# Second attention of a four-layer kernel: late row maxima, the doubts' branch, and a larger VectorE share of the first batch's counts

## The chip, the cores and the metric

The kernel runs on one core of a Trainium2 chip. The metric is the device time of one execution in microseconds (us), as the median of a few runs. TensorE is called PE here, VectorE DVE, ScalarE ACT, GpSimd POOL, SyncE SP.

## What is computed

Four layers, each attention then feed-forward, each with adaptive layer norm and a gated residual. The change lies in the attention of the second layer. It keeps, in every row of probabilities, the `k_keep` largest of 256, where `k_keep` is a number per head:

```python
q, k, v = (proj(Wq, bq), proj(Wk, bk), proj(Wv, bv))
scores = jnp.einsum('bhqd,bhkd->bhqk', q, k) / jnp.float32(np.sqrt(dh))
attn = jax.nn.softmax(scores, axis=-1)
k_keep = jnp.maximum(1, (L * (1.0 - sr)).astype(jnp.int32))
order = jnp.argsort(-attn, axis=-1)
rank = jnp.argsort(order, axis=-1)
keep = rank < k_keep[None, :, None, None]
w = jnp.where(keep, attn, jnp.float32(0.0))
w = w / (jnp.sum(w, axis=-1, keepdims=True) + 1e-10)
out = jnp.einsum('bhqk,bhkd->bhqd', w, v)
```

The batch is 8, there are 16 heads of 8 values, and 256 tokens; x is 8 x 256 x 128 in float32.

## The kernel before

The second attention, `l1_attn`, treats one batch entry after the other. Tokens lie on the 128 partitions, two tiles of them, so a batch has ROWS1 = 32 "rows", one for each head and token tile, each 128 x 256 probabilities. Instead of a sort it searches a threshold for each row and token. For batch b:

- PE computes the scores of head h (`l1_scores`, L1734) into one of three PSUM banks; DVE takes the negative row maximum (`l1_max`, L3092, tile `nmax`); ACT writes the exponentials and their sums (`l1_exps`, L4213). Scores of head h wait for the exponentials of head h - 3.
- After head 15's maximum, POOL makes the argument of a guessed threshold (`ask_start`, L1116), and ACT takes its exponential (`l1_start`, L4247).
- Three passes count in each row how many probabilities lie below the threshold (`QUICK_STEPS` = 3). DVE counts the first ROWS_DVE = 6 rows (`count_below`, L3105), ACT the other 26 with a Sign activation (`l1_count`, L4263). ACT's count of signs is in other units, so aim, window and the like (`keep_below`, `aim_below`, `per_count`, ...) are kept per row, with a factor 1 for DVE's rows and 2 for ACT's (`by_engine`). After each pass DVE moves the thresholds: `first_move` (L3113), `second_move` (`narrow`, L3125, and `between`), `settle_on` (`narrow`, `between` and some more). Each waits for ACT's counts, `counts_act`.
- DVE marks and counts what lies below the settled threshold in all 32 rows (`count_kept`, L3176), and works out how many of at most 8 are left over in each row. If a row has more, it is in doubt: `doubt` sums this, PE adds it over the partitions (`l1_doubt`), `ask_doubt` reads it (L3197), and `settle_doubt` branches on it (register load L3204, branch L3206, code after it from L3212). The branch skips a slow bisection, which these inputs do not need.
- POOL multiplies out candidates of a group of 4 rows (`candidates`), DVE takes the 8 largest of each (`largest_of`, L3220), and removes those that are too many (`all_but_past`, `mark`, L3232). PE turns kept probabilities to keys-first (`l1_turn_probs`, L1749 and L1750), ACT copies them (`l1_take_probs`, L4274), PE weighs the values (`l1_weigh`, L1762), ACT copies each four heads (`l1_take_quad`, L4278), and the batch is projected out.

Nothing is scheduled by a program: each engine has its own `l1_attn` with a loop `for n in range(-1, B)`, whose body interleaves by hand the batches n (marking and weighing), n + 1 (counting), n + 2 (scores and maxima) and n + 3 (norm and projection: `l1_norm`, L4222, `l1_turn`, L1676). `now(i)` says that batch i exists. Each engine works strictly in the order written, and waits on semaphores. In iteration -1 there is nothing to mark yet. `l1_gates` (L3041 to L3046) turns the modulation of all batches to gates, once. `l1_keep_counts` makes the limits per row, once, before the attention; its five instructions per engine share are L2954 to L2958.

DVE's loop, where row maxima and counts alternate:

```python
if now(n + 1):
    count_kept(n + 1, 8, 16)
if now(n + 2):
    l1_max(n + 2, 13)
    l1_max(n + 2, 14)
    l1_max(n + 2, 15)
if now(n + 1):
    count_kept(n + 1, 16, 24)
    count_kept(n + 1, 24, 32)
```

## Time and profile before

| | us |
|---|---|
| median of 3 runs | 2033.48 (2032.08 to 2033.51) |
| the profiled execution, its own time | 2029.82 |
| its span in the trace | 2028.1 |
| PE busy | 1561.3 (77%) |
| DVE busy | 1480.3 (73%) |
| ACT busy | 1123.5 (55%) |
| POOL busy | 877.5 (43%) |

Busy times are over the whole span, in which the second attention takes roughly from 489 to 1070 us. Rows give the start and the duration of an instruction in us from the span's start; in square brackets stands how long the engine was idle before it, and whose work ended that. "DVEq" and "ACTq" are the engines' sequencers, which handle branches, register loads and plain semaphore increments. Tile names are those of buffers that the program uses again: ACT's signs go to `rope_c` and `rope_s`, the counts of DVE to `scale_b`, `gate_b` and two more, and `weights`, `big`, `O` and `kT` hold probabilities.

### The profile page before, as it was taken

What the parts mean: (1) busy time and instruction counts of PE and PEld (TensorE: products, weight loads), DVE (VectorE), ACT (ScalarE), POOL (GpSimd) and SP (SyncE); (2) the same over time, 40 slices, a digit from 0 to 9 for tenths busy, and PEclk for the clock granted to TensorE, in tenths of its full rate; (3) what the DMA queues carried; (4) which work ended last, traced back from release to release, by engine and by line L of the source; (5) the groups of instructions that cost most, each with busy time, mean ns of one, the idle gap of its engine ahead of it and who ended that gap; (6) DMA issues with size and microseconds to landing.
All of it is one profiled execution on the core that took longest, in us unless ns stands there. A gap on an engine that the chain in (4) does not pass through costs nothing.

```text
span 2028.1 us, 38143 instructions
## 1 busy us (share of the span) xinstructions
PE 1561.3 (77%) x12256; PEld 997.2 (49%) x12256; DVE 1480.3 (73%) x4763; ACT 1123.5 (55%) x3354; POOL 877.5 (43%) x1162
## 2 busy tenths in 40 slices
PE   3878989987347777776669788527777799999978
PEld 3445667675223343343336556313443477777763
DVE  6678766555589999999998742458876778887657
ACT  2444444445988998999853333114452377666620
POOL 3333221124244554455333677666200377767610
PEclk8889999997567877878778989758896899999969
DMA  4111101003000000000001033222120000000000
GB/s 139 47 47 43 41 19 43 19 2 123 15 9 17 13 10 12 17 9 9 1 1 59 31 89 106 90 70 69 47 89 1 15 1 1 2 1 2 1 1 21
DMA packets 67303, 67.53 MB, mean 33 GB/s; under 512 B 9956, under 2 KB 58967, under 8 KB 66567
## 3 DMA queue, kind: packets, MB, share of 16 engines
q1 hardware_dynamic: 58930, 53.09, 8.0%
q0 software_dynamic: 5120, 10.50, 2.0%
q8 instruction: 101, 1.65, 0.3%
q10 hardware_dynamic: 3040, 1.38, 0.2%
q14 instruction: 112, 0.91, 0.1%
HBM read 30.41 MB, written 8.39 MB: 19 GB/s over the span
## 4 chain that ended last, share of the span: by engine, by line
PE 35%; ACT 22%; DVE 20%; issue 9%; POOL 6%; SPq 4%; ACTq 2%; DMA 1%; DVEq 0%; POOLq 0%; another core or an unknown queue 0%
ACT rope_s L4263 5%; ACT rope_c L4263 5%; POOL weights L1170 4%; SPq L694 4%; DVE weights L3176 3%; PE bank L2163 3%; PE bank L1556 3%; PE bank L2123 3%; ACT big L4485 3%; PE bank L1572 3%; DVE nmax L2731 2%; PE bank L2150 2%; PE bank L2111 2%; ACTq L4096 2%; DVE nmax L3092 2%
## 5 line engine op out<-in xcount | busy, mean ns | idle before, releaser
L2731 DVE TENSOR_REDUCE nmax<-bank 128x4 f32<-128x1024 f32 x144 | 175.9, 1222 | 51.5 <-PE bank L1336 48.4
L1762 PE MATMUL bank<-probsT,V 128*9 128x256 f32 x512 | 156.3, 450 | 28.4 <-ACT probsT L4274 28.3
L896 POOL TENSOR_TENSOR big<-big,rinv 128x512 f32<-128x512 f32 x128 | 131.6, 1048 | 45.7 <-DVE rinv L3795 45.7
L4078 ACT ACTIVATE feat_o<-bank 128x1024 f32<-128x1024 f32 x72 | 73.7, 1023 | 103.4 <-PE bank L1336 75.4
L4078 ACT ACTIVATE O<-bank 128x1024 f32<-128x1024 f32 x72 | 73.7, 1024 | 98.5 <-PE bank L1336 71.8
L3789 DVE TENSOR_REDUCE nmax<-bank 128x2 f32<-128x512 f32 x128 | 82.0, 683 | 58.1 <-PE bank L2123 58.1
L4485 ACT ACTIVATE big<-bank,nmax 128x256 f32<-128x256 f32 x256 | 117.6, 477 | 11.1 <-DVE nmax L3789 11.1
L4493 ACT ACTIVATE big<-bank 128x512 f32<-128x512 f32 x128 | 73.8, 614 | 68.8 <-PE bank L2150 68.8
L1750 PE MATMUL bank<-silu_b,weights 128*128 128x128 bf16 x464 | 108.6, 256 | 0.0
L1170 POOL DMA_INDIRECT weights<-h_rows,V x96 | 91.7, 955 | 32.2 <-issue 28.9
L1734 PE MATMUL bank<-qT 48*128 48x256 bf16 x256 | 53.9, 346 | 62.0 <-ACT weights L4213 42.5
L4274 ACT ACTIVATE probsT<-bank 128x512 f32<-128x512 f32 x128 | 76.1, 601 | 39.4 <-PE bank L1750 21.3
L3092 DVE TENSOR_REDUCE nmax<-bank 128x2 f32<-128x512 f32 x128 | 84.1, 681 | 9.8 <-PE bank L1734 9.8
L1762 PEld LDWEIGHTS bank<-probsT,V 128*9 128x9 f32 x512 | 39.0, 98 | 98.8 <-ACT probsT L4274 40.1
L2163 PE MATMUL bank<-big,V 128*64 128x256 f32 x512 | 69.4, 390 | 16.8 <-ACT V L4500 15.7
L3565 DVE TENSOR_TENSOR O<-O,bank 128x512 f32<-128x512 f32 x24 | 16.5, 688 | 90.0 <-ACT O L4409 88.4
L1749 PE MATMUL bank<-const,big 128*128 128x128 f32 x256 | 68.1, 347 | 17.4 <-ACT probsT L4274 11.4
L4137 ACT ACTIVATE hid<-bank,weights 128x256 f32<-128x256 f32 x128 | 52.5, 470 | 48.6 <-PE bank L1556 48.5
L2150 PE MATMUL bank<-const,big 128*128 128x128 f32 x512 | 75.0, 279 | 2.5 <-POOL big L896 1.7
L1178 POOL DMA_INDIRECT weights<-y_rows,V x64 | 62.0, 968 | 29.7 <-issue 16.9
L1360 PE MATMUL bank<-big 57*128 57x128 bf16 (+1 forms) x512 | 41.7, 266 | 39.6 <-DVE nmax L2731 22.6
L2150 PEld LDWEIGHTS bank<-const,big 128*128 128x128 f32 x512 | 56.6, 141 | 28.9 <-issue 16.5
(821 smaller groups left out, 5094.5 us busy)
## 6 DMA issues: line engine op xcount, KB each, us to landing
qT<-parts SPq DMA_DIRECT2D x276, 32.0 KB
big<-V SPq DMA_DIRECT2D x192, 32.0 KB
y_rows<-weights SPq DMA_DIRECT2D x24, 256.0 KB, 2.2
big<-parts SPq DMA_DIRECT2D x180, 32.0 KB
weights<-in_weights_l_ffn SPq DMA_DIRECT2D x1, 4832.0 KB, 14.4
weights<-in_weights_l_attn SPq DMA_DIRECT2D x1, 3904.0 KB, 13.2
qT<-V SPq DMA_DIRECT2D x96, 32.0 KB
weights<-in_weights_l_ffn SPq DMA_DIRECT2D x1, 2860.0 KB, 11.4
```

Of the source, the lines that this page charges most:

```text
L896: nc.gpsimd.tensor_tensor(row, row, rinv[:, h % H, :].unsqueeze(2).to_broadcast([P, T, S]), ALU.mult).then_inc(scaled.sem, 1)
L1170: nc.gpsimd.indirect_dma_start(gathered[i % RING1][:, t, :], None, h_rows, bass.IndirectOffsetOnAxis(ap=token_of[:, at:at + 1], axis=0)).t ...
L1750: last = mm(pb[6 + h % 2][:, at], unkept(b, g)[:, 2 * (h % 2) + t, keys], minus_two, start=False, stop=True)
L1762: last = mm(pb[1][part, 0:S].rearrange("p (t n) -> p t n", t=T), values_of(b, k)[:, h * wide:(h + 1) * wide], by_keys[:, k], start=k == 0, ...
L2150: last = nc.tensor.transpose(pb[TURN_BANKS3[h % 2]][:, k * S + t * P:k * S + (t + 1) * P], probs3[h % PROBS3][:, t * S + k * P:t * S + (k ...
L2163: last = mm(pb[7][HD3 * i:HD3 * (i + 1), w * S:(w + 1) * S], values3(q, k, 2 * w + i), probsT3[(4 * q + 2 * w + i) % TURNED3][:, k * S:(k ...
L2731: V_.tensor_reduce(to, scored.rearrange("p (i a n) -> p i a n", i=HPG, n=n), AX.X, ALU.max, negate=True).then_inc(score_max.sem, 1)
L3092: V_.tensor_reduce(nmax[:, h, :], tiles(pb[2 + n % 3]), AX.X, ALU.max, negate=True).then_inc(max_ready.sem, 1)
L3789: V_.tensor_reduce(nmax[:, h % H, :], tiles(pb[h % 4][:]), AX.X, ALU.max, negate=True).then_inc(max_ready.sem, 1)
L4078: nc.scalar.activation(turned_probs[n % TURNS], turned_scores, ACT.Exp).then_inc(turned_exp.sem, 1)
L4263: nc.scalar.activation(signs[signed[0] % len(signs)], row_of(b, j), ACT.Sign, bias=at[:, 0, j:j + 1], scale=-1.0, accum_out=at[:, 1, j:j + ...
L4485: last = nc.scalar.activation(probs3[h % PROBS3][:, t * S:(t + 1) * S], pb[h % 4][:, t * S:(t + 1) * S], ACT.Exp, bias=nmax[:, h % H, t:t ...
```

## The change

- DVE counts 14 rows for batch 0 (`ROWS_FIRST`) and 6 for the others; ACT counts the rest, 18 and 26. The limits per row are first made for 14 and 18, and once batch 0 has settled, `resplit_rows` makes them again for 6 and 26: ten instructions, each waiting for the one before. POOL makes `per_count` again in `start_ends` of batch 1.
- `l1_gates` moves from before the loop to between the second count of batch 0 and its `second_move`.
- The maximum of head 0 of batch n + 2 moves from behind the first `mark` to between the two `largest_of` that precede the branch of the doubts; PE computes these scores right after `l1_doubt`.
- The maxima of heads 13, 14 and 15 are spread over `count_kept`, four rows of it before each.
- PE's `l1_turn` of batch n + 3 follows the first `l1_turn_probs`.
- ACT's first count from row 20 on is in one piece, and `l1_norm` follows it.

```diff
@@ -52,7 +52,7 @@
 ROWS1 = H * T
-ROWS_DVE = 6
+ROWS_DVE, ROWS_FIRST = 6, 14
 GROUPS = ROWS1 // 4
@@ -65,7 +65,7 @@
 BISECT_RAISES = 5
-KEEP_STEPS = 32
+KEEP_STEPS, RESPLIT_STEPS = 32, 10
@@ -484,7 +484,8 @@
         window_below, per_count = (masks_flat[:, ROWS1 * i:ROWS1 * (i + 1)] for i in range(2))
-        by_engine = ((slice(0, ROWS_DVE), 1.0), (slice(ROWS_DVE, ROWS1), 2.0))
+        rows_dve = lambda b: ROWS_DVE if b else ROWS_FIRST
+        by_engine = lambda b: ((slice(0, rows_dve(b)), 1.0), (slice(rows_dve(b), ROWS1), 2.0))
         silu1 = tail1[:, 0:B * P].rearrange("p (b n) -> p b n", b=B)
@@ -1086,7 +1087,7 @@
                 link(nc.gpsimd.memset(start_half[:], 0.5))
-                for of, each in by_engine:
+                for of, each in by_engine(0):
                     link(nc.gpsimd.memset(per_count[:, of], DAMPED / (PSEUDO * each)))
@@ -1119,6 +1120,10 @@
                 step = guesses[b % 3][:, 1, :]
+                if b == 1:
+                    for of, each in by_engine(b):
+                        link(nc.gpsimd.memset(per_count[:, of], DAMPED / (PSEUDO * each)))
+                    pool.wait_ge(keep_count, KEEP_STEPS + RESPLIT_STEPS)
                 pool.wait_ge(start_ready.sem, start_ready(ph, b, 1))
@@ -1806,18 +1811,19 @@
                         l1_doubt(n)
+                    if now(n + 2):
+                        l1_scores(n + 2, 0)
                     if now(n - 1):
                         l1_turn_quad(n - 1, QUADS - 1)
                     if now(n + 2):
                         l1_values(n + 2)
-                    if now(n + 3):
-                        l1_turn(n + 3)
-                    if now(n + 2):
-                        l1_scores(n + 2, 0)
                         l1_scores(n + 2, 1)
                         l1_scores(n + 2, 2)
                     if now(n):
                         l1_turn_probs(n, 0)
+                    if now(n + 3):
+                        l1_turn(n + 3)
+                    if now(n):
                         l1_turn_probs(n, 1)
@@ -2914,6 +2920,28 @@
+            def split_rows(b, then):
+
+                for of, each in by_engine(b):
+                    then(V_.tensor_scalar(keep_below[:, of], keep[:, of], -each, float(S), ALU.mult, ALU.add))
+                    then(V_.tensor_scalar(aim_below[:, of], aim[:, of], -each, float(S), ALU.mult, ALU.add))
+                    then(V_.tensor_scalar(under_below[:, of], aim_below[:, of], -each * PSEUDO, None, ALU.add))
+                    then(V_.tensor_scalar(over_below[:, of], aim_below[:, of], each * PSEUDO, None, ALU.add))
+                    then(V_.memset(window_below[:, of], each * each * ((LEFT / 2) ** 2 + 0.3)))
+
+            def resplit_rows():
+
+                dve.wait_ge(mid_ready.sem, mid_ready("l1_attn", 0, QUICK_STEPS))
+                n = [KEEP_STEPS]
+
+                def then(ins):
+                    n[0] += 1
+                    ins.then_inc(keep_count, 1)
+                    dve.wait_ge(keep_count, n[0])
+
+                split_rows(1, then)
+                assert n[0] == KEEP_STEPS + RESPLIT_STEPS, f"RESPLIT {n[0]}"
+
             def l1_keep_counts(ph="l1_attn"):
@@ -2950,12 +2978,7 @@
                 then(V_.tensor_scalar(aim[:], keep[:], -LEFT / 2, None, ALU.add))
-                for of, each in by_engine:
-                    then(V_.tensor_scalar(keep_below[:, of], keep[:, of], -each, float(S), ALU.mult, ALU.add))
-                    then(V_.tensor_scalar(aim_below[:, of], aim[:, of], -each, float(S), ALU.mult, ALU.add))
-                    then(V_.tensor_scalar(under_below[:, of], aim_below[:, of], -each * PSEUDO, None, ALU.add))
-                    then(V_.tensor_scalar(over_below[:, of], aim_below[:, of], each * PSEUDO, None, ALU.add))
-                    then(V_.memset(window_below[:, of], each * each * ((LEFT / 2) ** 2 + 0.3)))
+                split_rows(0, then)
                 aim_of = aim[:].rearrange("p (h t) -> p h t", t=T)[:, :, 0]
@@ -3096,10 +3119,10 @@
                     dve.wait_ge(start_ready.sem, start_ready(ph, b, 1))
-                    dve.wait_ge(probs_ready.sem, probs_ready(ph, b, (ROWS_DVE + 1) // 2))
+                    dve.wait_ge(probs_ready.sem, probs_ready(ph, b, (rows_dve(b) + 1) // 2))
                 else:
                     dve.wait_ge(mid_ready.sem, mid_ready(ph, b, it))
-                for j in range(ROWS_DVE):
+                for j in range(rows_dve(b)):
                     if j >= len(flags):
@@ -3290,19 +3313,19 @@
                 l1_spread(1)
                 l1_guess(1)
-                l1_gates()
                 for n in range(-1, B):
                     if now(n + 1):
                         count_below(n + 1, 0)
                     if now(n):
                         ask_doubt(n)
                         largest_of(n, 0)
+                    if now(n + 2):
+                        l1_max(n + 2, 0)
+                    if now(n):
                         largest_of(n, 1)
                         settle_doubt(n)
                         all_but_past(n, 0)
                         mark(n, 0)
-                    if now(n + 2):
-                        l1_max(n + 2, 0)
                     if now(n + 1):
                         first_move(n + 1)
@@ -3332,6 +3355,8 @@
                         count_below(n + 1, 1)
+                        if n < 0:
+                            l1_gates()
                         second_move(n + 1)
@@ -3365,6 +3390,8 @@
                     if now(n + 1):
                         settle_on(n + 1)
+                    if n + 1 == 0:
+                        resplit_rows()
                     if now(n + 2):
                         l1_max(n + 2, 9)
@@ -3374,14 +3401,19 @@
                         l1_max(n + 2, 12)
                     if now(n + 1):
-                        count_kept(n + 1, 8, 16)
+                        count_kept(n + 1, 8, 12)
                     if now(n + 2):
                         l1_max(n + 2, 13)
+                    if now(n + 1):
+                        count_kept(n + 1, 12, 16)
+                    if now(n + 2):
                         l1_max(n + 2, 14)
+                    if now(n + 1):
+                        count_kept(n + 1, 16, 20)
+                    if now(n + 2):
                         l1_max(n + 2, 15)
                     if now(n + 1):
-                        count_kept(n + 1, 16, 24)
-                        count_kept(n + 1, 24, 32)
+                        count_kept(n + 1, 20, 32)
                     if now(n + 3):
                         l1_guess(n + 3)
@@ -4256,7 +4288,7 @@
                     act.wait_ge(probs_ready.sem, probs_ready(ph, b, (end - 1) // T + 1))
-                for j in range(first, end):
+                for j in range(max(first, rows_dve(b)), end):
                     signed[0] += 1
@@ -4286,11 +4318,9 @@
                     if now(n + 1):
-                        l1_count(n + 1, 0, 20, 21)
+                        l1_count(n + 1, 0, 20, ROWS1)
                     if now(n + 3):
                         l1_norm(n + 3)
-                    if now(n + 1):
-                        l1_count(n + 1, 0, 21, ROWS1)
                     if now(n):
```

(Left out: the start number of steps in `l3_route`, which follows the ten new ones.) Three places in the order of DVE's instructions, before and after. First iteration -1, from the guess of batch 1 on: L3078 is its last instruction, L3041 to L3046 (now L3064 to L3069) are the gates, L3105 (now L3128) is one counted row, and `nmax` a maximum. Before:

```order
L3078 TENSOR_SCALAR hb<-hb 128x32
L3041 TENSOR_SCALAR hid<-bank 128x1024
L3042 TENSOR_SCALAR hid<-bank 128x1024
L3044 TENSOR_TENSOR hid<-bank,hid 128x1024
L3046 SCALAR_TENSOR_TENSOR probs<-hid 128x1024
L3105 TENSOR_SCALAR scale_b,front_n<-big,front_n 128x256
L3105 TENSOR_SCALAR gate_b,front_n<-big,front_n 128x256
```

And now, the end of the second count, the gates, and the second `narrow`:

```order
L3128 TENSOR_SCALAR gate_sign,small<-big,small 128x256
L3128 TENSOR_SCALAR scale_b,small<-big,small 128x256
L3128 TENSOR_SCALAR gate_b,small<-big,small 128x256
L3064 TENSOR_SCALAR hid<-bank 128x1024
L3065 TENSOR_SCALAR hid<-bank 128x1024
L3067 TENSOR_TENSOR hid<-bank,hid 128x1024
L3069 SCALAR_TENSOR_TENSOR probs<-hid 128x1024
L3148 TENSOR_TENSOR small<-small,routes 128x32
L3149 TENSOR_TENSOR small<-small,routes 128x32
```

The gates have left the place ahead of the first count and stand ahead of the second `narrow`; each count has 14 such rows instead of 6. Next the last maxima in iteration 3; L3164 (now L3187) ends `settle_on`, L3176 (now L3199) is `count_kept`. Before:

```order
L3164 COPY_PREDICATED small<-small 128x32
L3092 TENSOR_REDUCE nmax<-bank 128x2 x2
L3176 TENSOR_SCALAR weights,small<-big,small 128x256 x8
L3092 TENSOR_REDUCE nmax<-bank 128x2 x2
L3176 TENSOR_SCALAR weights,small<-big,small 128x256 x8
L3092 TENSOR_REDUCE nmax<-bank 128x2 x3
L3176 TENSOR_SCALAR weights,small<-big,small 128x256 x12
L3176 TENSOR_SCALAR O,small<-big,small 128x256 x4
```

And now:

```order
L3187 COPY_PREDICATED small<-small 128x32
L3115 TENSOR_REDUCE nmax<-bank 128x2 x2
L3199 TENSOR_SCALAR weights,small<-big,small 128x256 x8
L3115 TENSOR_REDUCE nmax<-bank 128x2 x2
L3199 TENSOR_SCALAR weights,small<-big,small 128x256 x4
L3115 TENSOR_REDUCE nmax<-bank 128x2
L3199 TENSOR_SCALAR weights,small<-big,small 128x256 x4
L3115 TENSOR_REDUCE nmax<-bank 128x2
L3199 TENSOR_SCALAR weights,small<-big,small 128x256 x4
L3115 TENSOR_REDUCE nmax<-bank 128x2
```

Of the last three maxima, each now stands behind four more counted rows than the one before it, and head 15's behind row 19. Last, the branch of the doubts in iteration 3; MAX is `largest_of`, L3204 (now L3227) the register load. Before:

```order
L3197 CAST doubts_i<-bank 1x1
L3199 MEMSET gap 128x1
L3220 MAX small<-hid 128x8 x8
L3204 TENSOR_LOAD doubts_i
L3204 ISA x2
L3206 COMPARE_AND_BRANCH
```

And now:

```order
L3220 CAST doubts_i<-bank 1x1
L3222 MEMSET gap 128x1
L3243 MAX small<-hid 128x8 x4
L3115 TENSOR_REDUCE nmax<-bank 128x2
L3243 MAX small<-hid 128x8 x4
L3227 TENSOR_LOAD doubts_i
L3227 ISA x2
L3229 COMPARE_AND_BRANCH
```

A maximum has come between the two groups of four MAX.

## Rows read from the trace of the kernel before

**Rows 1.** The page: busy us, share of the span, instructions, of two engines.
```profile
PE 1561.3 (77%) x12256; PEld 997.2 (49%) x12256; DVE 1480.3 (73%) x4763; ACT 1123.5 (55%) x3354; POOL 877.5 (43%) x1162
```
**Rows 2.** Timeline of ACT: `l1_start` and first signs (start, us, what, idle before).
```profile
637.16 0.23 ACT L4247 ACTIVATE front_n<-neg_mid 128x32 f32<-128x32 f32 x1 [0.62 <-POOL neg_mid L1117]
...
776.95 0.51 ACT L4263 ACTIVATE rope_c<-big,front_n 128x256 bf16<-128x256 f32 x1
...
777.46 0.49 ACT L4263 ACTIVATE rope_s<-big,front_n 128x256 bf16<-128x256 f32 x1
...
984.24 0.23 ACT L4247 ACTIVATE front_n<-neg_mid 128x32 f32<-128x32 f32 x1 [0.61 <-POOL neg_mid L1117]
```
**Rows 3.** Busy time by engine in two windows of one period.
```profile
776.69:832.29 55.60, 42.44 (x209) 22.25 (x208) 50.80 (x218) 54.56 (x209) 28.88 (x38) 0.72 0.04 12
832.29:845.78 13.49, 10.52 (x62) 4.99 (x62) 13.16 (x57) 9.71 (x37) 4.50 (x4) 0.87 0.05 13
```
Columns: stretch, its length, busy time (instructions) of PE, PE's weight loads, DVE, ACT and POOL, granted clock, DMA share, GB/s.

**Rows 4.** Timeline of ACT in the same period: its waits.
```profile
786.28 0.38 ACT L4278 ACTIVATE V<-bank 128x256 f32<-128x256 f32 x1 [0.57 <-PE bank L1762]
...
794.98 0.60 ACT L4274 ACTIVATE probsT<-bank 128x512 f32<-128x512 f32 x1 [0.17 <-ACT rope_s L4263]
...
840.22 0.47 ACT L4213 ACTIVATE weights<-bank,nmax 128x256 f32<-128x256 f32 x1 [2.22 <-DVE nmax L3092]
...
844.62 0.47 ACT L4213 ACTIVATE O<-bank,nmax 128x256 f32<-128x256 f32 x1 [1.49 <-DVE nmax L3092]
...
846.53 0.23 ACT L4247 ACTIVATE front_n<-neg_mid 128x32 f32<-128x32 f32 x1 [0.62 <-POOL neg_mid L1117]
```
**Rows 5.** Timeline of DVE and POOL around the last maxima of that period.
```profile
843.90 1.88 DVE L3092 TENSOR_REDUCE nmax<-bank 128x2 f32<-128x512 f32 x3
845.69 0.47 DVE L3176 TENSOR_SCALAR_CACHE_REDUCE weights<-big,small 128x256 bf16<-128x256 f32 x1
...
845.86 0.25 POOL L1116 TENSOR_TENSOR neg_mid<-hb,nmax 128x32 f32<-128x32 f32 x1 [1.64 <-DVE nmax L3092]
...
846.09 0.47 DVE L3176 TENSOR_SCALAR_CACHE_REDUCE weights<-big,small 128x256 bf16<-128x256 f32 x1
```
**Rows 6.** Timeline of DVE: `first_move`, second and third `narrow` of that period.
```profile
794.88 0.19 DVE L3113 TENSOR_TENSOR front_n<-front_n,routes 128x32 f32<-128x32 f32 x1 [1.38 <-ACTq L4267]
...
812.40 0.19 DVE L3125 TENSOR_TENSOR small<-small,routes 128x32 f32<-128x32 f32 x1 [0.56 <-ACTq L4267]
...
832.29 0.18 DVE L3125 TENSOR_TENSOR small<-small,routes 128x32 f32<-128x32 f32 x1
```
**Rows 7.** Timeline of DVE: behind the branch, iterations 1 and 3, and head 0.
```profile
651.84 0.43 DVE L3212 TENSOR_TENSOR weights<-const,small 128x256 f32<-128x256 f32 x1 [2.02 <-DVEq L3209]
...
790.51 0.43 DVE L3212 TENSOR_TENSOR weights<-const,small 128x256 f32<-128x256 f32 x1 [1.16 <-DVEq L3209]
...
792.82 0.68 DVE L3092 TENSOR_REDUCE nmax<-bank 128x2 f32<-128x512 f32 x1
```
**Rows 8.** Timeline of DVE and ACT in iterations -1 and 0.
```profile
514.05 1.22 DVE L3041 TENSOR_SCALAR hid<-bank 128x1024 f32<-128x1024 f32 x1 [2.96 <-PE bank L1664]
...
536.85 0.19 DVE L3125 TENSOR_TENSOR small<-small,routes 128x32 f32<-128x32 f32 x1 [4.65 <-ACTq L4267]
...
553.73 0.19 DVE L3125 TENSOR_TENSOR small<-small,routes 128x32 f32<-128x32 f32 x1 [3.78 <-ACTq L4267]
...
581.82 0.42 DVE L3212 TENSOR_TENSOR weights<-const,small 128x256 f32<-128x256 f32 x1 [1.65 <-DVEq L3209]
...
585.84 0.60 ACT L4274 ACTIVATE probsT<-bank 128x512 f32<-128x512 f32 x1 [2.13 <-PE bank L1750]
```
**Rows 9.** Timeline of DVE: ten limits per row in `l1_keep_counts`, and the next.
```profile
444.47 0.17 DVE L2954 TENSOR_SCALAR routes<-keep 128x6 f32<-128x6 f32 x1
...
446.43 0.17 DVE L2960 TENSOR_SCALAR gate_b<-aim 128x16 f32<-128x16 f32 x1
```

2 lines of the change are left out of this document (1 added, 1 removed).

## Prediction

> **What bounds the kernel now.** I began with the page [rows 1]: VectorE is busy 73% of the span and ScalarE 55%, which says nothing about the second attention, since both figures are means over nine stages. So I went to the instructions in order of time. `l1_start` (line 4247) runs once per batch, and its rows give the period: from 637.16 us (batch 2) to 984.24 us (batch 7) there are five batches, (984.24 - 637.16) / 5 = 69.4 us each [rows 2]. Next I cut one period into three windows [rows 3]. From `l1_start` of one batch (776.69) to VectorE's third `narrow` (832.29), ScalarE is busy 54.56 of 55.60 us. Its only long wait there is 0.57 us for PE's last weighing [rows 4]; the rest are the 0.17 us pauses at the end of its counts. From 832.29 to 845.78 VectorE is busy 13.16 of 13.49 us, while ScalarE waits 2.22 and 1.49 us for row maxima. Then GpSimd's `ask_start` waits for the last maximum, takes 0.6 us, and `l1_start` follows at 846.53 [rows 4, 5].
>
> So the loop that sets the period is: last row maximum (VectorE), `ask_start` (GpSimd), `l1_start` and all three passes of counting (ScalarE), third `narrow` and everything up to the last row maximum (VectorE). Its parts are 55.6 + 13.5 + 0.75 (845.78 to 846.53) = 69.8 us for this batch. VectorE has slack outside its part of the loop: 1.38 us before `first_move`, 0.56 us before the second `narrow`. Only at the third `narrow`, 832.29, do both arrive together; no wait stands in its row [rows 6].
>
> **The change, part by part.** The sum is against the profiled execution, 2029.82 us (span 2028.1); the runs' median, 2033.48, lies 3.7 us above, and I add that at the end.
>
> 1. *Late maxima.* Before, the maxima of heads 13, 14 and 15 ran together at 843.90 to 845.78, before row 16 of `count_kept` [rows 5]. Now maximum 15 stands behind rows 16 to 19 as well. The rows of that count start 0.40 us apart (845.69, 846.09 [rows 5]), so four make 1.61 us. Everything that hangs on maximum 15 comes 1.61 us later: `ask_start`, `l1_start`, and with them ScalarE's 55 us. The head 13 maximum comes earlier by 1.6 us, so ScalarE's wait before `l1_exps` of head 13 (1.49 us) goes; but behind it stands only `l1_take_quad`, and then `l1_start`, so that time reappears as a wait for `l1_start`: 0.62 before, about 3.7 us now. VectorE loses nothing at first, it does the same work in another order, but its slack behind it fills with waiting for ScalarE. The late starts are those of batches 2 to 7, six of them (iterations 0 to 5): 6 x 1.61 = **+9.7 us**. That of batch 1 is also late, by 1.61 less what part 2 gains, but there ScalarE has 2.13 us to spare at 585.84 [rows 8], which covers it.
>
> 2. *First batch.* VectorE counts 14 rows instead of 6, ScalarE 18 instead of 26. ScalarE's rows start 0.50 us apart (776.95, 777.46 [rows 2]), so a pass costs it 4.0 us less; VectorE's 8 more rows cost 3.2 us where it waited 4.65 and 3.78 us [rows 8]. I followed it through. Pass one: VectorE needs no longer wait for `l1_gates` (514.05 after 2.96 us of waiting, then four instructions of 1.22 us, 4.9 us in all [rows 8]); it counts at once from 511.1, where that wait began, so `first_move` falls at about 517.4, after 14 rows and a maximum, where before the gates alone lasted until 518.9. Pass two: ScalarE counts until about 528.4, but VectorE counts until 527.9 and then does the 4.9 us of `l1_gates`, so the second `narrow` starts at 532.8 instead of 536.85. Pass three: with 2.1 us for `narrow` and `between` and 5.7 for 14 rows VectorE is done at 540.7, and only then come the statistics and maximum 5, out at 542.3, for which ScalarE now waits some 5 us in the middle of its count; its last 14 rows then take it to about 550.5. The third `narrow` starts there instead of at 553.73: 3.2 us are left. Then come the ten new instructions of `resplit_rows`, each behind the last; the same ten took 1.96 us (444.47 to 446.43 [rows 9]), 2.05 with the first wait. What is left is **-1.15 us**. It passes through VectorE to the first `mark`, and from there to ScalarE, which waits for it [rows 8]. The two memsets and the wait added to GpSimd's `start_ends` of batch 1 are free: the next to need it is `first_move`, 10 us on.
>
> 3. *Branch of the doubts.* The maximum of head 0 moves from behind the first `mark` to between the two `largest_of` (0.6 us, 792.82 [rows 7]). The first `mark`, for which PE's `l1_turn_probs` and then ScalarE wait, comes 0.6 us later, unless the branch hides it. Branch and register load cost VectorE 1.16 us here after the eighth MAX8, and 2.02 us in batch 1 [rows 7]. No row tells whether the load starts while MAX8 still runs. Bounds: if it does, the extra maximum lies in its shadow and the cost is 0. If not, 0.6 us in iterations 0, 1 and 5, where ScalarE waits for PE at this point, and the 0.6 less some 0.3 of slack in 2 to 4 (from the first instruction behind the branch to ScalarE took 585.84 - 581.82 = 4.02 us where it waited [rows 8]; 790.51 + 4.02 = 794.53, against 794.98 found [rows 4, 7]): 2.7 us. The rows favour neither, I take half: **+1.4 us**.
> The Trainium skill (TensorE: Matmul & The Clock Gate, on engine queue depths) gives VectorE a strictly ordered queue of 8, so that the sequencer can be ahead of the engine by about those MAX8. By that rule the load is under way early, and this term would be 0 and the sum 1.4 us lower; no row here shows it.
>
> 4. *ScalarE's count in one piece.* `l1_norm` moves behind the first pass. The counts are out 0.87 us earlier, `first_move` waits less, but ScalarE's work up to the second `narrow` is the same, and VectorE waits there for the rest: 0. If VectorE were the bound, this would be a gain (below).
>
> 5. *PE.* Scores of batch n+2 no longer stand behind `l1_turn`, which waits for the branch; ScalarE's first exponentials never waited for them (the maximum is out at 793.5, and ScalarE is still at its count and then at `l1_take_probs` until 795.5 [rows 4, 7]), so 0. `l1_turn` now follows `l1_turn_probs` of head 0 and may hold `l1_take_normed` by 0 to 0.2 us a batch, 1 us in all; I take 0, as ScalarE's copy of the probabilities (0.60 us [rows 4]) covers the two transposes.
>
> Sum: +9.7 - 1.15 + 1.4 = +9.9 us, 2039.7 us for a profiled execution, **2043.4 us** for the median of the runs.
>
> **Rivals.**
> - *VectorE sets the period* (faster). Then the maxima's place is free, the count in one piece takes 0.87 us off the wait at `first_move` in each of six batches, and the branch hides 0.6 us in seven: 5.2 + 4.2 + 1.15 = 10.6 us less, 2022.9 for the median. It decides if ScalarE has room for 1.6 us between `l1_start` and the third `narrow`. For it: VectorE arrives there without waiting in one batch. Against it: ScalarE is busy 98% of that window, and VectorE waits for it twice a batch. Chance 0.08.
> - *The lateness is absorbed* (no change). VectorE's waits, 1.38 + 0.56 us, are more than 1.61, and if ScalarE could catch up inside a period, only the first batch's -1.15 would show: 2032.3. Against it: an engine that works in order and is 98% busy catches up only by its 1.0 us of waits, most of which move with it. Chance 0.10.
> - *The branch gets dearer* (slower still). The gap after MAX8 was 1.65 and 2.02 us in the first two batches and 1.16 in the fourth, with the same instructions each time [rows 7, 8]. If the shifted code makes it 2.02 everywhere, that is 0.86 us more in six batches, less 0.3 of slack in half of them: +4.3 us, 2047.7. Chance 0.12. The Trainium skill (Runtime: NRT & Kernel Launch, on instruction fetch) says that a taken branch to a target outside the fetched pages stalls for a fetch, which would make such a gap hang on where code lies; the scatter here agrees with it but does not prove it.
> - *The first batch does not gain at all*: its part is 1.15 us, and the forecast's range holds it.
>
> **How the numbers follow.** A measurement of this kernel can tell 0.2%, about 4 us, from no change. My forecast has 0.70, and the dearer branch 0.12: 0.82 for slower. The absorbed case gives 0.10 for within 0.2%, the VectorE case 0.08 for faster. The forecast's own bounds: down 1.4 (hidden branch) and one late start absorbed, 1.6, so 2040.4; up 1.3 + 1.0 and 0.6, so 2046.3. The base adds uncertainty: the profiled time lay 3.7 us below the median, so an offset may be as small as 0 and the low end 2036.7. With the dearer branch above, the range is 2036.5 to 2048; it leaves out the faster and the absorbed case, 0.18.
>
> **What would show it.** In the changed profile: rows of `l1_start` about 71.0 to 71.5 us apart instead of 69.4, with some 3.7 us of ScalarE waiting for GpSimd before each; VectorE waiting over 1.5 us more per batch in sum before `first_move`, `narrow` and the reading of the doubts; third `narrow` of batch 0 near 550.5, and the maximum after it near 555.4; the gap behind the last MAX8 of batch 1 on at 1.2 us (not hidden) or 0.6 us (hidden). I am wrong if the starts stay 69.4 us apart, or if ScalarE, started later, still finishes its third pass in time.

## The result, and the profile after

| | before | after |
|---|---|---|
| median of the runs, same chip | 2034.49 (2032.08 to 2037.95, 6 runs) | 2042.45 (2038.67 to 2047.55, 6 runs) |
| span of the profiled execution | 2028.1 | 2039.9 |

The ratio after to before is 1.0044, with a 95% interval of 1.0033 to 1.0055. The kernel got slower by some 8 to 9 us. The forecast was 9.9 us above a profiled execution of before, which gave 2039.7 for a profiled execution (2041.67 came out) and 2043.4 for the median. The page of after answers to [rows 1]:

```profile
PE 1560.6 (77%) x12256; PEld 996.6 (49%) x12256; DVE 1497.8 (73%) x4821; ACT 1112.7 (55%) x3306; POOL 878.3 (43%) x1164
```

Busy shares have not moved, and ScalarE even does 11 us less (24 counts of two instructions each fewer, in the first batch). What moved is the wait ahead of `l1_start`. The timeline of ACT after, against [rows 2]:

```profile
639.55 0.23 ACT L4279 ACTIVATE front_n<-neg_mid 128x32 f32<-128x32 f32 x1 [3.01 <-POOL neg_mid L1118]
...
783.12 0.23 ACT L4279 ACTIVATE front_n<-neg_mid 128x32 f32<-128x32 f32 x1 [2.50 <-POOL neg_mid L1118]
...
995.87 0.23 ACT L4279 ACTIVATE front_n<-neg_mid 128x32 f32<-128x32 f32 x1 [3.08 <-POOL neg_mid L1118]
```

Five periods take 356.32 us, 71.26 each instead of 69.42, and the wait for GpSimd is 2.5 to 3.1 us instead of 0.62 (the forecast had 3.7). Both come out of one place, which the timelines of DVE and POOL show (compare [rows 5]):

```profile
850.64 0.68 DVE L3115 TENSOR_REDUCE nmax<-bank 128x2 f32<-128x512 f32 x1
851.25 0.47 DVE L3199 TENSOR_SCALAR_CACHE_REDUCE weights<-big,small 128x256 bf16<-128x256 f32 x1
...
852.84 0.68 DVE L3115 TENSOR_REDUCE nmax<-bank 128x2 f32<-128x512 f32 x1
```
```profile
853.60 0.25 POOL L1117 TENSOR_TENSOR neg_mid<-hb,nmax 128x32 f32<-128x32 f32 x1 [3.24 <-DVE nmax L3115]
```

From head 14's maximum to head 15's it is 2.20 us, one maximum and four counted rows, where there were 0.6 us before. The windows of after follow: five periods, then, as in [rows 3], `l1_start` to the third `narrow` and from there to the last maximum (that of after is taken at its end, 853.53). Behind them stands the same five-period window of before:

```profile
639.55:995.87 356.32, 255.60 (x1348) 130.33 (x1348) 327.46 (x1360) 320.67 (x1227) 165.43 (x214) 0.79 0.04 11
783.12:838.42 55.30, 38.98 (x206) 20.17 (x204) 50.40 (x210) 54.55 (x209) 28.95 (x38) 0.81 0.04 12
838.42:853.53 15.11, 12.63 (x70) 6.11 (x70) 14.78 (x64) 9.83 (x37) 4.50 (x4) 0.77 0.04 11
```
```profile
637.16:984.24 347.08, 255.13 (x1349) 129.86 (x1348) 322.05 (x1360) 320.25 (x1227) 165.22 (x214) 0.79 0.04 11
```

The stretch up to the third `narrow` is as long as before (55.30 and 55.60 us, ScalarE busy 54.55 and 54.56). The one behind it went from 13.49 to 15.11 us: 1.62 us, where the working had 1.61. ScalarE's busy time over five periods is the same, 320.67 and 320.25 us; VectorE's is 5.4 us more, which the forecast had not (see the last section). Last, whose waits ScalarE has in these five periods, of before and of after (us in total, times, longest):

```profile
ACT big L4213 <- DVE nmax L3092: 7.4, 4, 2.2
ACT weights L4213 <- DVE nmax L3092: 6.6, 3, 2.2
ACT O L4213 <- DVE nmax L3092: 4.5, 3, 1.5
ACT front_n L4247 <- POOL neg_mid L1117: 3.7, 6, 0.6
ACT probsT L4274 <- PE bank L1750: 1.7, 2, 1.1
```
```profile
ACT front_n L4279 <- POOL neg_mid L1118: 17.3, 6, 3.1
ACT weights L4245 <- DVE nmax L3115: 6.6, 3, 2.2
ACT big L4245 <- DVE nmax L3115: 4.4, 2, 2.2
ACT O L4245 <- PE bank L1755: 2.4, 3, 0.9
ACT probsT L4306 <- PE bank L1755: 1.7, 2, 1.2
...
ACT big L4245 <- PE bank L1755: 1.3, 2, 0.7
ACT next_feat L4267 <- PE bank L1681: 0.9, 3, 0.3
```

The wait of `l1_start` grew by 13.6 us over the six starts counted; ScalarE's waits for row maxima fell from 18.5 to 11.0 us at the same time, since head 13's maximum comes earlier. The waits of `O` and `big` for PE are new, 3.7 us together: where ScalarE waited 1.49 us for a maximum it now waits 0.6 to 0.95 us for PE, and so the wait of `l1_start` is less than the forecast's 3.7 us. The last line is new too: three waits of 0.3 us for `l1_turn`.

### The profile page after: what moved, and what is told of

It reads as the page before. It is cut to its first block, busy times and chain, and to the rows that moved or that the text cites. A ratio compares the mean times of both kernels' runs of the same rounds, so it can differ in the third digit from the quotient of the medians.

```text
span 2039.9 us, 38150 instructions
## 1 busy us (share of the span) xinstructions
PE 1560.6 (77%) x12256; PEld 996.6 (49%) x12256; DVE 1497.8 (73%) x4821; ACT 1112.7 (55%) x3306; POOL 878.3 (43%) x1164
## 4 chain that ended last, share of the span: by engine, by line
PE 35%; DVE 22%; ACT 22%; issue 10%; POOL 6%; ACTq 3%; SPq 2%; DMA 1%; DVEq 0%; POOLq 0%
ACT rope_s L4295 5%; ACT rope_c L4295 5%; POOL weights L1175 4%; DVE weights L3199 3%; PE bank L2169 3%; PE bank L1561 3%; PE bank L2129 3%; ACT big L4515 3%; PE bank L1577 3%; ACTq L4128 2%; SPq L695 2%; DVE nmax L3115 2%; PE bank L2156 2%; PE bank L1390 2%; PE bank L2117 2%
## 5 line engine op out<-in xcount | busy, mean ns | idle before, releaser
L1754 PEld LDWEIGHTS bank<-const,big 128*128 128x128 f32 x256 | 45.1, 176 | 72.7 <-issue 36.6
L2156 PEld LDWEIGHTS bank<-const,big 128*128 128x128 f32 x512 | 56.6, 141 | 28.9 <-issue 16.5
```

The source lines that it names most:

```text
L1754: mm(pb[6 + h % 2][:, at], row_of(b, 2 * h + t)[:, keys], C("ident"), start=True, stop=False, is_transpose=True)
L2156: last = nc.tensor.transpose(pb[TURN_BANKS3[h % 2]][:, k * S + t * P:k * S + (t + 1) * P], probs3[h % PROBS3][:, t * S + k * P:t * S + (k ...
```

## The experiments

All but e2 and e12 are edits of the changed kernel, those two are edits of the kernel before. The diffs below are shortened to the calls that move, without their `if now(...)`. A "start" is a start of `l1_start`, the first interval is the time from start 0 to start 1, and a period is the time from one start to the next. The table has, from one profile of each kernel, the distance from `l1_start` of batch 0 to that of batch 7, and the mean of the last five periods. These are free of what happens ahead of the attention: its first `l1_start` fell anywhere from 502.3 to 511.0 us in these kernels.

| run | ratio to before (95%) | median | start 0 to 7 | period |
|---|---|---|---|---|
| before | 1 | | 479.56 | 69.42 |
| after | 1.0044 (1.0033 to 1.0055) | 2042.45 | 489.35 | 71.26 |
| e1 | 1.0003 (0.9990 to 1.0016) | 2034.18 | 480.98 | 70.14 |
| e2 | 1.0045 (1.0028 to 1.0062) | 2042.62 | 489.81 | 70.91 |
| e3 | 0.9978 (0.9966 to 0.9990) | 2029.80 | 474.74 | 69.24 |
| e4 | 1.0095 (1.0068 to 1.0121) | 2051.95 | 500.62 | 72.70 |
| e5 | 1.0049 (1.0032 to 1.0067) | 2044.53 | 489.01 | 71.24 |
| e6 | 1.0045 (1.0027 to 1.0063) | 2042.82 | 491.75 | 71.64 |
| e7 | 1.0050 (1.0032 to 1.0068) | 2041.51 | 489.18 | 71.27 |
| e8 | 1.0021 (1.0005 to 1.0036) | 2036.24 | 477.34 | 69.12 |
| e9 | 0.9962 (0.9948 to 0.9977) | 2027.88 | 475.24 | 69.30 |
| e10 | 0.9944 (0.9927 to 0.9960) | 2023.94 | 471.54 | 68.76 |
| e11 | 1.0086 (1.0070 to 1.0103) | 2053.36 | 496.69 | 72.65 |
| e12 | 0.9974 (0.9962 to 0.9985) | 2029.82 | 475.63 | 69.00 |

The kernel before had a median of 2033.29 beside e1 to e4, 2032.85 beside e5 to e8, and 2035.79 beside e9 to e12.

**e1, the changed kernel with the maxima put back.**

```diff
-count_kept(n + 1, 8, 12);  l1_max(n + 2, 13)
-count_kept(n + 1, 12, 16); l1_max(n + 2, 14)
-count_kept(n + 1, 16, 20); l1_max(n + 2, 15)
-count_kept(n + 1, 20, 32)
+count_kept(n + 1, 8, 16)
+l1_max(n + 2, 13); l1_max(n + 2, 14); l1_max(n + 2, 15)
+count_kept(n + 1, 16, 24); count_kept(n + 1, 24, 32)
```

> The changed kernel with the maxima of heads 13 to 15 back in one piece before row 16 of count_kept, all else as changed. Theory (the last maximum starts ScalarE's 55 us, nothing absorbs it): starts of ScalarE's first count back to about 69.4 to 69.7 us apart instead of 71.3, time 9.7 us below the changed kernel, about 2033, a little under the kernel before. Rival (the loss is in the other edits: PE's order, the branch, the count in one piece): starts stay 71 us apart and the time stays above 2040.

Measured: 2034.18, no change against before; the wait ahead of `l1_start` is back at 0.62 us. So nearly the whole loss hangs on the place of the maxima. Between starts 0 and 7 the late maxima cost 8.37 us here, against 10.25 in e2. The first interval is 2.42 us shorter than before (60.89 against 63.31), and yet start 0 to 7 is 1.4 us longer: the first batch's gain is given back on the way. The largest part, 2.46 us, is lost in the period in which VectorE stalls for 2.00 us behind the branch (iteration 4, see e7). The rest goes with waits of 0.3 to 0.6 us of ScalarE for PE, some of them where before had none. The granted clock over the five periods was 0.75 here and 0.79 in before, which is a second candidate for these waits (see the last section).

**e2, the kernel before with the late maxima alone** (the reverse of the diff above).

> The kernel before with the late maxima alone. Theory: 6 x 1.61 = 9.7 us above the kernel before, about 2044, starts 71.0 us apart. Rival (late maxima are absorbed, or hurt only together with the other edits): within 2 us of the kernel before, starts 69.4 apart.

Measured: 2042.62, as slow as the changed kernel. The period is 70.91 us, 1.49 above before. The late start of batch 1 (1.61 us) was not covered by ScalarE's 2.13 us to spare, as the working had it: at start 2 the delay is 2.79 us. VectorE's own path had moved as well. Counted from start 0, the doubts of batch 0 are read at 73.75 us (before 72.48), and ScalarE still waits 1.73 us for PE. The reading in e2, and in before:

```profile
581.61 0.14 DVE L3197 CAST doubts_i<-bank 1x1 int32<-1x1 f32 x1
```
```profile
577.16 0.14 DVE L3197 CAST doubts_i<-bank 1x1 int32<-1x1 f32 x1
```

One start on ACT's timeline, and the window over the five periods:

```profile
643.13 0.23 ACT L4252 ACTIVATE front_n<-neg_mid 128x32 f32<-128x32 f32 x1 [3.10 <-POOL neg_mid L1117]
```
```profile
643.13:997.67 354.54, 260.35 (x1348) 132.70 (x1348) 327.48 (x1360) 320.31 (x1226) 165.43 (x214) 0.77 0.04 11
```

VectorE's extra 5.4 us of busy time are here too (327.48), so they too belong to the maxima.

**e3, the maxima earlier than ever.**

```diff
 count_kept(n + 1, 8, 12)
 l1_max(n + 2, 13); l1_max(n + 2, 14); l1_max(n + 2, 15)
 count_kept(n + 1, 12, 32)
```

> The changed kernel with maxima 13, 14 and 15 together behind row 11 of count_kept, four rows earlier than in the kernel before and eight earlier than now. Theory: each row moved is worth 0.40 us a batch in both directions, so 6 x 3.2 = 19 us below the changed kernel, about 2023, starts 67.8 us apart. Rival (VectorE becomes the bound as soon as ScalarE starts earlier than in the kernel before): no more than 2 us below the kernel before, starts 69 us or more apart, ScalarE waiting for VectorE's threshold moves instead.

Measured: 2029.80, ratio 0.9978: faster than before, but by much less than eight rows a batch would be. ScalarE no longer waits at `l1_start`; it waits for PE at its first copy of probabilities (the waits of ACT, 633.93 to 980.11, and one of them on its timeline):

```profile
ACT probsT L4300 <- PE bank L1755: 8.9, 5, 3.0
```
```profile
791.11 0.60 ACT L4300 ACTIVATE probsT<-bank 128x512 f32<-128x512 f32 x1 [1.28 <-PE bank L1755]
```

The loop has changed hands. It now runs from the last maximum through the rest of `count_kept`, the doubts, their branch and the first `mark` (VectorE) to PE and ScalarE. Against the changed kernel the early maxima are worth 14.6 us between starts 0 and 7, about 2 us a batch of the 3.2 that the eight rows weigh.

**e4, the maxima four rows later still** (`count_kept` 16 to 24 ahead of maximum 15 in place of 16 to 20).

> The changed kernel with the maximum of head 15 another four rows later (behind row 23). Theory: another 6 x 1.61 = 9.7 us, about 2052, starts 72.9 us apart. Rival (most of the loss is a fixed cost of splitting the maxima, or of something else): within 3 us of the changed kernel.

Measured: 2051.95, and a period of 72.70. From start 0 to 7 it takes 11.27 us more than the changed kernel, 1.61 for each of seven batches; e2 took 10.25 more than before, 1.46 for each. On this side the price is nearly linear. One start:

```profile
641.38 0.23 ACT L4279 ACTIVATE front_n<-neg_mid 128x32 f32<-128x32 f32 x1 [4.69 <-POOL neg_mid L1118]
```

**e5, head 0's maximum back behind the first `mark`.**

```diff
 largest_of(n, 0)
-l1_max(n + 2, 0)
 largest_of(n, 1); settle_doubt(n); all_but_past(n, 0); mark(n, 0)
+l1_max(n + 2, 0)
```

> The changed kernel with the maximum of head 0 back behind the first mark (PE's order stays). Theory (the branch's register load runs while the eight MAX8 do, so the extra maximum is hidden): gap behind MAX8 back from 0.7 to 1.2-1.3 us, time from the CAST of the doubts to the code behind the branch unchanged at 4.3 us, starts 71.2 us apart as now, time within 2 us of the changed kernel (2042). Rival (the maximum costs its 0.6 us before mark): mark 0.6 us earlier in each batch, up to 3 us less.

Measured: the periods are those of the changed kernel within 0.2 us each, start 0 to 7 is 489.01 against 489.35. In iterations 1 to 5 VectorE's gap behind the eighth MAX8 is 1.14 to 1.30 us in place of 0.70 to 0.79. Iteration 2 in e5, then iteration 3 in the changed kernel:

```profile
724.69 0.14 DVE L3220 CAST doubts_i<-bank 1x1 int32<-1x1 f32 x1 [0.81 <-remote]
...
728.85 0.42 DVE L3235 TENSOR_TENSOR weights<-const,small 128x256 f32<-128x256 f32 x1 [1.14 <-DVEq L3232]
```
```profile
791.92 0.15 DVE L3220 CAST doubts_i<-bank 1x1 int32<-1x1 f32 x1
...
793.55 0.67 DVE L3115 TENSOR_REDUCE nmax<-bank 128x2 f32<-128x512 f32 x1
...
796.28 0.43 DVE L3235 TENSOR_TENSOR weights<-const,small 128x256 f32<-128x256 f32 x1 [0.74 <-DVEq L3232]
```

From the reading of the doubts (`CAST`) to the first instruction behind the branch it is 4.16 us without the maximum and 4.36 with it. Of its 0.6 us, 0.4 are hidden. The remaining 0.2 hardly show, since ScalarE's path is the longer one in most periods; in the three in which ScalarE waits for PE at its first copy, e5 is 0.22, 0.09 and 0.11 us shorter.

**e6, no larger share for batch 0** (six rows for all batches, no `resplit_rows`; `l1_gates` stays where the change put it).

> The changed kernel with 6 rows for VectorE in the first batch too, and no second making of the limits; the gates stay where the change put them. Theory 1 (moving the gates gives the first batch's gain; the larger share and its ten instructions cancel out): third narrow of batch 0 about 46.5 us after the first start, first maximum behind it as early as now (49.4 us after the first start), time within 1 us of the changed kernel. Theory 2 (the larger share is what gains): that maximum 2 us later. A stall of 1.8 us that now stands behind the branch in iteration 4 (waiting for nothing the profile shows) should move or go if it hangs on where code lies, as VectorE's program is shorter by 34 instructions there.

Measured: 2042.82, like the changed kernel. The first interval is 63.15 us; e2, which has the late maxima and nothing else, has 64.92, the changed kernel 62.49. So moving the gates, together with the small edits of PE's and ScalarE's order, which e6 keeps, gives 1.77 us, and the larger share adds 0.66. The later periods are 71.64 us, 0.38 above the changed kernel's; the granted clock over them was 0.74, against 0.79 there (see the last section). VectorE's stall of the changed kernel (see e7) stands in iteration 5 here, with 0.75 us. The third `narrow` in e6, then in the changed kernel, where the wait before it is hardly shorter:

```profile
554.33 0.19 DVE L3144 TENSOR_TENSOR small<-small,routes 128x32 f32<-128x32 f32 x1 [3.78 <-ACTq L4293]
```
```profile
551.06 0.19 DVE L3148 TENSOR_TENSOR small<-small,routes 128x32 f32<-128x32 f32 x1 [3.43 <-ACTq L4299]
```

**e7, 24 tiny memsets ahead of the loop**, which move VectorE's code.

```diff
 for h in range(H):
     l1_max(0, h)
+for _ in range(24):
+    linkup()
+    link(V_.memset(gap[:], 0.0))
+linkup()
```

> The changed kernel with 24 tiny memsets more on VectorE, where it waits for PE before the first batch's guess (2.9 us idle, so they cost under 0.5 us). Theory (the stall of 1.8 us in iteration 4 is the loading of code after the taken branch, and hangs on the program's position): it moves to another place or goes, and with it up to 1.3 us of the time. Rival (it belongs to what the instruction waits for): it stays at the same instruction with 1.8 us.

It tests a stall that the changed kernel shows in iteration 4 and the kernel before nowhere in this stretch. First the changed kernel, then e7:

```profile
867.39 0.42 DVE L3235 TENSOR_TENSOR weights<-const,small 128x256 f32<-128x256 f32 x1 [0.70 <-DVEq L3232]
869.61 0.23 DVE L3249 SCALAR_TENSOR_TENSOR small<-weights,small 128x64 f32<-128x64 f32 x1 [1.79 <-issue]
```
```profile
1065.27 0.23 DVE L3249 SCALAR_TENSOR_TENSOR small<-weights,small 128x64 f32<-128x64 f32 x1 [1.72 <-issue]
```

With the code shifted, the stall leaves iteration 4 and stands in iteration 7. In e1, e3 and e4, which have as many VectorE instructions ahead of it as the changed kernel, it stands at the same instruction of iteration 4, though that comes at 865.16, 858.24 and 875.14 us. So it goes with the place in the code, not with the time or with what the instruction waits for. Start 0 to 7 is 489.18 against 489.35, though: ScalarE's wait of 1.18 us behind the stall is gone, but waits of 0.3 to 0.6 us for PE have come in other places.

**e8, the next batch's count behind the mark**, so that VectorE reaches the branch 2.4 us sooner (from e3's kernel).

```diff
-count_below(n + 1, 0)
-ask_doubt(n); largest_of(n, 0); l1_max(n + 2, 0); largest_of(n, 1)
+largest_of(n, 0); largest_of(n, 1); ask_doubt(n); l1_max(n + 2, 0)
 settle_doubt(n); all_but_past(n, 0); mark(n, 0)
+count_below(n + 1, 0)
```

> The kernel with early maxima, and VectorE's first count of batch n+1 moved behind the first mark of batch n; the two largest_of come before the reading of the doubts. With early maxima alone ScalarE waited 1.1 to 3.0 us a batch for PE's first transposes of probabilities, which wait for that mark. Theory (VectorE's path to the mark sets the period there): mark up to 2.4 us earlier, ScalarE's wait goes, starts 68 us or less apart instead of 69.2, time 4 to 8 us below 2029.8. Rival (the register load then shows in full, some 3 us behind the CAST, and eats what is gained): 2029 to 2032.

Measured: 2036.24, slower than e3 by about 0.4%. The periods are no longer than in e3 (69.12 and 69.24 us). Start 0 to 7 is 2.60 us longer, and the whole loss is in the first interval, 62.87 against 59.30 us. It comes from the edit and not from the branch: in iteration -1 the count now stands behind the maximum of head 0, and VectorE waits for its scores before it counts anything (first line below). Why the medians differ by more than that (6.4 us) stays open. In the later periods little work is left behind the reading of the doubts, and the gap grows to what the work had covered, so that next to nothing is gained. Iteration 3 (second and third line):

```profile
519.11 0.69 DVE L3115 TENSOR_REDUCE nmax<-bank 128x2 f32<-128x512 f32 x1 [3.33 <-PE bank L1739]
...
791.34 0.13 DVE L3220 CAST doubts_i<-bank 1x1 int32<-1x1 f32 x1
...
795.33 0.42 DVE L3235 TENSOR_TENSOR weights<-const,small 128x256 f32<-128x256 f32 x1 [2.96 <-DVEq L3232]
```

3.99 us lie between the two, about as in e5 (4.16) and the changed kernel (4.36). Register load and branch are a latency of about 4 us from the reading on, and the work put behind it is free up to that.

**e9, e3 with `l1_turn` and `l1_norm` at their old places.**

```diff
 # PE
+l1_turn(n + 3)
 l1_turn_probs(n, 0)
-l1_turn(n + 3)
 # ACT
-l1_count(n + 1, 0, 20, ROWS1)
+l1_count(n + 1, 0, 20, 21)
 l1_norm(n + 3)
+l1_count(n + 1, 0, 21, ROWS1)
```

> The changed kernel with three edits: maxima 13 to 15 directly behind row 11 (as in the run e3), PE's l1_turn back ahead of the first l1_turn_probs, and ScalarE's l1_norm back inside the first count. In e3 VectorE's path to the first mark set the period, with ScalarE waiting for PE before its first copy. Theory: the order of PE is worth 0.3 us a batch at most and only where ScalarE gets to l1_take_normed early; the norm inside the count makes VectorE wait at first_move longer, which is free only while VectorE is not the bound. So starts 69.0 to 69.5 us apart, median within 2 us of 2030. Rival: with VectorE the bound, the norm inside the count costs its 0.87 us a batch, starts 70 us apart, 2035.

Measured: 2027.88, periods 69.30 us: as e3, within what can be told (the intervals of the ratios overlap). Together the two moves are worth nothing. e11 takes them apart.

**e10, the doubts added up earlier** (from e9).

```diff
 # PE, in iteration n
 l1_weigh(n, 13)
+l1_doubt(n + 1)     # the one at the loop's start stays for batch 0 alone
 l1_weigh(n, 14)
 # DVE
+ask_doubt(n)
 count_below(n + 1, 0)
-ask_doubt(n)
-largest_of(n, 0); l1_max(n + 2, 0); largest_of(n, 1)
+largest_of(n, 0); largest_of(n, 1)
 settle_doubt(n); all_but_past(n, 0); mark(n, 0)
+l1_max(n + 2, 0)
```

> The kernel of e9, and the branch's input earlier: PE adds the doubts of batch n+1 ahead of weighing head 14 of batch n, so that VectorE can read them before its count of the next batch's first six rows; the register load then has the six rows and eight MAX8 (5 us) to run behind, and the head 0 maximum goes back behind the first mark. Theory (load and branch take about 4.2 us from the reading on, whatever lies between): the gap behind the last MAX8 falls from 0.7 to about 0.2 us and the maximum's 0.6 us leaves the path, so starts about 68.2 us apart and a median of 2023 to 2026. Rival: PE waits for the count of doubts ahead of weighing heads 14 and 15, which delays the last quad that ScalarE copies behind its starts; then starts 69 to 70 us apart and 2029 or more.

Measured: 2023.94, ratio 0.9944 (0.9927 to 0.9960), the lowest median of all and faster than both kernels (the interval overlaps that of e9). DVE's timeline in iteration 3, and one line of ACT's waits over the five periods:

```profile
775.92 0.15 DVE L3221 CAST doubts_i<-bank 1x1 int32<-1x1 f32 x1 [0.28 <-PE bank L1784]
...
781.59 0.43 DVE L3236 TENSOR_TENSOR weights<-const,small 128x256 f32<-128x256 f32 x1 [0.25 <-DVEq L3233]
```
```profile
ACT V L4305 <- PE bank L1767: 4.7, 5, 1.3
```

Six rows and eight MAX8 now stand behind the reading, and only 0.25 us of the gap are left. The period fell by 0.54 us against e9, not by the 1.1 that were expected. The stall in iteration 4 (1.23 us) is no reason, since e9 has one of 2.09 us there. The last line names one: ScalarE waits up to 1.3 us for the last weighing, 4.7 us in five periods against 0.6 in e9. That is the rival's mechanism, though its time did not come.

**e11, `l1_turn` alone at its old place.**

```diff
+l1_turn(n + 3)
 l1_turn_probs(n, 0)
-l1_turn(n + 3)
```

> The changed kernel with PE's l1_turn back ahead of the first l1_turn_probs, nothing else. Theory: ScalarE's three waits of 0.3 us for PE before l1_take_normed go, but ScalarE is on the path of the loop, so the starts are at most 0.3 us closer, 71.0 us apart, and the median 1 to 2 us below 2042. Rival (the forecast's zero): no change, 2042. Rival on the other side: the scores of head 0 and the first copy of probabilities come 0.5 us later where ScalarE already waits for PE, 2044.

Measured: 2053.36 us, 0.4% slower than the changed kernel, and a period of 72.65. Only the sign of the third expectation fits, and not its price or its reason. The chain can be read off PE's and ACT's timelines in iteration 3:

```profile
802.01 0.69 PE L1681 MATMUL bank<-const,xb 128*128 128x128 f32 x2 [6.85 <-ACT xb L4253]
802.49 0.42 PE L1754 MATMUL bank<-const,weights 128*128 128x128 f32 x1
```
```profile
801.08 0.88 ACT L4253 ACTIVATE xb<-x,moments,rstd 128x128 f32<-128x128 f32 x2 [0.17 <-ACT rope_s L4294]
804.01 0.60 ACT L4305 ACTIVATE probsT<-bank 128x512 f32<-128x512 f32 x1 [2.06 <-PE bank L1755]
```

`l1_turn` needs ScalarE's `l1_norm`, and that now stands behind the whole first count. PE, in strict order, waits 6.85 us for it in front of the turning of probabilities that were ready, and then ScalarE waits 2.06 us for PE. The changed kernel's two edits are one: with `l1_norm` late, `l1_turn` has to stand behind `l1_turn_probs` (changed kernel), or both stay early (before, e9).

**e12, the kernel before with the early maxima alone.**

> The kernel before with maxima 13, 14 and 15 directly behind row 11 instead of row 15, nothing else. Theory: ScalarE's part of the loop gets 1.6 us shorter per batch, but VectorE's path to the first mark has only about 1.4 us of slack in the kernel before, and its gap behind the last MAX8 is 1.16 us, not 0.7 as in the changed kernel; so VectorE takes over, starts 68.7 to 69.4 us apart instead of 69.4, median 2028 to 2033. It tells what e3 owes to the changed kernel's other edits: if they are worth nothing here, e12 is 2.4 us (the first batch) above e3's 2029.8. Rival: the whole 1.6 us shows, 67.8 us apart, 2024.

Measured: 2029.82, ratio 0.9974, a period of 69.00. So e3 owes its gain to the early maxima; the rest of the change adds nothing that can be told in the medians. Its first interval is 2.41 us shorter than that of e12 (59.30 and 61.71), and 1.52 of these are lost again by start 7. ScalarE's share of the loop got 1.6 us shorter, the period 0.42.

## Why the prediction was right, and where not

The time, its sign and its place were right, and so was the mechanism of the main term. That the sum came out so close, 9.9 us where start 0 to 7 grew by 9.79, was luck: 1.4 us for the branch did not come, the first batch gained 1.3 more than forecast, the main term was 0.55 too small, and 2.0 us came that no term had. By the terms:

- **Late maxima, +9.7.** Confirmed. Start 0 to 7 grew by 10.25 us in e2, where this is the only edit; e4 gives 11.27 for four rows more. Putting it back (e1) takes the loss away. Six starts of 1.61 us was not quite the count: all seven intervals grew, by 1.46 on average, since the late start of batch 1 was not covered.
- **First batch, -1.15.** The size was off: the first interval is 2.43 us shorter than e2's. The step that failed is the third pass, which I had end at 550.5 with 3.2 us gained; against the first `l1_start` it ended 4.5 us sooner (551.06 - 506.52 = 44.54, before 49.05). Most of that was there by the second `narrow`, which I had at 28.1 us from the first `l1_start` and which came at 27.02 (533.54 - 506.52): VectorE's second count was over sooner than I had it. From the third `narrow` to the maximum behind `resplit_rows` it took 4.91 us, before 2.83, so its ten instructions cost 2.08 us, as worked out (2.05), and the wait of ScalarE for maximum 5 is there (5.32 us, forecast 5). The gates' move gives 1.77 of it (e6, with the small edits), the 14 rows 0.66.
- **Branch, +1.4.** Wrong in size, 0 would have been nearly right: e5 puts the maximum back, and start 0 to 7 changes by 0.34 us. The lower bound held, "if the load starts while MAX8 still runs". The Trainium skill (TensorE: Matmul & The Clock Gate, engine queue depths) gives VectorE a strictly ordered queue of 8, by which this term was to be 0; e5 and e8 agree with it.
- **ScalarE's count in one piece, 0, and PE's order, 0.** The sum is right, the working was not. I priced the two apart and did not see that the first is free only because of the second: e11, which takes them apart, is 7.3 us slower between starts 0 and 7. Also, the pair costs 0.3 us in three of five periods at `next_feat`; the working had said that ScalarE's copy covers it.
- **VectorE loses nothing.** Wrong, without consequence: it is busy 5.4 us more (last section), in time that it would have waited.
- **The bound.** It was shown to be ScalarE's path from `l1_start`, and each step later costs nearly its full length, 1.46 (e2) to 1.61 us (e4) of 1.61. What I underrated is how close the other path lay. ScalarE's waits for PE at its first copy in before (2.13, 0.60 and 1.07 us in three of seven periods) were a sign: e3 and e12 gain 0.2 to 0.4 us a batch of the 1.6 on offer before the branch's path takes over.

Between starts 0 and 7 the terms add up: 10.25 (e2) - 2.43 = 7.8 us, against 9.79 measured. The missing 2.0 lies behind the first batch. Against e2, the period from start 3 is 1.41 us longer (four waits of ScalarE for PE, 0.30 to 0.57 us each), that from start 5 is 1.17 us longer (the stall of 1.79 us, and 1.18 us of ScalarE waiting behind it), and the last is 0.97 us shorter. What brings these waits stays open: e7, without the stall in iteration 4, has other such waits and the same sum, and the granted clock is a candidate too (last section).

The rivals: that VectorE sets the period was wrong for this change, and is right for the opposite one (e3). The absorbed case is excluded by e2. The dearer branch did not come: the gap is smaller in every iteration of the changed kernel but the last two, in which no maximum stands before it. Its reason may be real, one instruction further on: the stall of 1.79 us behind the taken branch that moves with the code (e7). The Trainium skill (Runtime: NRT & Kernel Launch, instruction fetch) says that a taken branch to a target outside the fetched pages stalls for a fetch, and the moving stall agrees with it; what was fetched no row shows.

## What to carry to other kernels

Where two engines hand a loop to each other, the place of the one instruction that releases the other engine was worth nearly its full delay once per turn here, however much slack the busy shares suggest; try it in both directions, and expect the gain to stop at the second-longest path. Price edits together when one engine's wait is another's output: a step moved later on one engine (`l1_norm`) makes its reader (`l1_turn`) a plug in that engine's queue. A branch on data cost about 4 us here, counted from the reading of its input, so read early and put useful work behind it.
